# Attention in a transformer layer: tile 10 of the steady heads made in two parts, and one low part moved from GpSimd to VectorE

## The chip, the core and the metric

One core of one Trainium2 chip runs the whole program in one launch. The metric is the device time in microseconds (us). PE is TensorE, DVE is VectorE, ACT is ScalarE, POOL is GpSimd, and SP is the engine whose queue issues most of the transfers. The engines run beside each other, and only semaphores order them.

## The reference, cut to what matters

The layer is causal attention with 16 heads of width 32 over 2048 tokens, followed by a mixture of 16 experts. The change touches the attention alone:

```python
qkv = x @ W_qkv.T                       # x is layer-normed, 2048 x 512
q, k, v = jnp.split(qkv, 3, axis=-1)    # 16 heads of 32
attn = jnp.einsum('bhqd,bhkd->bhqk', q, k) * SCALE
attn = jnp.where(causal[None, None], attn, -jnp.inf)
probs = jax.nn.softmax(attn, axis=-1)
out = jnp.einsum('bhqk,bhkd->bhqd', probs, v)
```

All of it is float32.

## The kernel before, in words

PE multiplies in the format fp32r, which keeps fewer bits of a number than float32 does. A number x is therefore written as a high part (x copied to fp32r) and a low part (x minus its high part), and the products of the parts are summed.

**The tiles of a head.** A head has NS = 20 tiles (`S_TILES`, line 526). A tile is a pair of 128-key blocks against one block of 512 queries (j). Block j = 0 has tiles 0 and 1, j = 1 has 2 to 5, j = 2 has 6 to 11, j = 3 has 12 to 19. The last tile of a block (1, 5, 11, 19) covers 2x256 numbers in each partition, all others 2x512. Tile 10 is one that the causal mask cuts, so that its second key block needs only 384 of the 512 queries on PE.

**What happens to a tile.**
- PE makes the scores (`scores`, line 900: L911, and L915 for the mask) into one of two PSUM places.
- ACT takes the exponential into `prob` (L752), one of RING = 5 places.
- The high part `prob_hi` is made by ACT (L739), or by DVE (L796) for the tiles in `HI_DVE`.
- The low part `prob_lo` is made by POOL (L717) for the tiles in `LO_POOL`, otherwise by DVE (L803).
- PE multiplies both parts with the values (`times_v`, L893) LAG = 4 steps after the scores, so tile t's values stand in step t + 4, and those of tiles 16 to 19 in steps 0 to 3 of the next head. PE does the product with the high part first and the one with the low part after it.
- A tile in `WHOLE` has neither part: PE multiplies `prob` itself in float32 (L884).
- When all tiles of a query block are summed, ACT copies the sum out (`copy_out`, L733), PE turns it, DVE reads it (`read_out`, L788 and L789), and POOL scales it and stores it (`store_out`, L708). DVE's read of one block waits until POOL has stored the block before it.

**Beside it**, PE and DVE work on the next head's row maxima. PE makes 40 pieces of scores (L852, L855) into two PSUM places, and DVE reduces each (L767). `PIECES_AT` says how many pieces stand in each step: none in steps 0 to 4, two or three in each later one.

**Order.** Each engine has its own loop over the 20 steps, and its order is fixed by that code. In step t, DVE does the first pieces, then the high and low part of tile t - 1 if they are its own, then further pieces, then what `SHARED_AT` names for the step. So the low part of tile 17 would stand in DVE's step 18, ahead of the read of block 2 and of the two pieces of step 19. POOL goes through its own tiles in order, with the four stores between: block 3 of the head before after tile 6, block 0 after tile 9, block 1 after tile 15, block 2 after tile 18. Heads 0 to 14 use the sets `WHOLE`, `HI_DVE` and `LO_POOL` (head 0 written out, 1 to 14 in a loop). Head 15 has sets of its own, which are not changed.

Of the kernel before, what the change touches and what calls it, by code (L numbers as in the profile page):

```python
# [526 lines left out]
NS = len(S_TILES)  # L527
# [24 lines left out]
FW = VW + 1  # L552


WHOLE, WHOLE_LAST = {10}, {7, 17, 18}
HI_DVE, HI_DVE_LAST = {2, 3}, {1, 2, 3, 4, 5, 8, 9, 11, 13, 15, 19}
LO_POOL, LO_POOL_LAST = set(range(NS)) - {0, 1, 2, 18, 19} - WHOLE, {0}

def load_projection(sp, flat, wproj_dram, wgate_dram, landed):

# [1591 lines left out]
```

## Time and profile before

| | |
|---|---|
| median of three runs | 1682.74 us (1682.65 to 1682.8) |
| profiled execution | 1683.45 us, its span 1681.3 us |
| busy: PE, DVE, ACT, POOL | 1609.8, 1189.7, 1146.0, 907.0 us |
| granted TensorE clock, mean | 0.983 |
| POOL's low parts (L717) | 211 in 467.0 us, 2245 ns each on average |
| DVE's low parts (L803) | 91 of both sizes, in 111.3 us |

Attention runs from about 158 us to about 780 us of the span. A steady head takes 38.5 us there. Shares over the whole span say little about it, since the second half of the span is the expert stage, so the rows below are of steady heads.

### The profile page before, as it was taken

Reading aid. Unit: us, or ns where it says so; the run is one execution under the profiler, and the core shown is the slowest. Engines: PE = TensorE matmul, PEld = TensorE weight load, DVE = VectorE, ACT = ScalarE, POOL = GpSimd, SP = SyncE. Lnnn points to the kernel's source line nnn. Section 1 sums busy time; section 2 is a strip of 40 time slices with the busy share of each in tenths; the row PEclk is TensorE's granted clock in tenths of the full one; section 3 lists DMA queues with packets and bytes.
Section 4 is the critical chain, followed back from the end, with each engine's and each line's share of the span. In section 5 each row is a group of like instructions: output and inputs, shape, how many; then the busy total and the mean of one; then the engine's idle time right before and its main releaser. Section 6 shows DMA issues by size and latency. Waiting matters only on the chain.

```text
span 1681.3 us, 30901 instructions
## 1 busy us (share of the span) xinstructions
PE 1609.8 (96%) x9214; PEld 1360.1 (81%) x9214; DVE 1189.7 (71%) x2394; ACT 1146.0 (68%) x1729; POOL 907.0 (54%) x761
## 2 busy tenths in 40 slices
PE   7999999999999999999977999999999999999991
PEld 7988777777777777776756999999999999999991
DVE  6427888888888888887787667566665566556555
ACT  3222899999989999986776566566665565556554
POOL 2321788888888887874663443434343434343432
PEclk9999999999999999999988999999999999999996
DMA  8676221111111122212716898888887887788747
GB/s 254 188 222 186 63 67 51 50 50 50 50 50 50 51 71 71 59 48 88 267 48 237 234 283 243 230 257 237 240 254 216 223 259 213 205 253 235 195 111 219
DMA packets 103474, 268.21 MB, mean 160 GB/s; under 512 B 21129, under 2 KB 38921, under 8 KB 96073
## 3 DMA queue, kind: packets, MB, share of 16 engines
q1 hardware_dynamic: 77929, 204.64, 36.8%
q0 software_dynamic: 25440, 62.27, 18.2%
q8 instruction: 54, 0.88, 0.2%
q14 instruction: 51, 0.42, 0.1%
HBM read 190.55 MB, written 59.27 MB: 149 GB/s over the span
## 4 chain that ended last, share of the span: by engine, by line
PE 86%; DVE 6%; DMA 3%; issue 2%; ACT 1%; POOL 1%; SPq 1%; DVEq 0%; ACTq 0%; POOLq 0%
PE p_prj L91 26%; PE a_op L893 13%; PE a_sp L911 8%; PE a_mp L852 8%; PE p_at_ps L91 7%; PE p_logit_ps L91 7%; PE e_qp L91 5%; PE p_ht_ps L2031 3%; PE p_at_ps L2054 2%; PE e_vp L91 2%; PE a_op L884 2%; PE a_mp L855 1%; PE a_sp L915 1%; PE a_shared L870 1%; DVE r_lane_hot L1718 1%
## 5 line engine op out<-in xcount | busy, mean ns | idle before, releaser
L717 POOL TENSOR_TENSOR prob_lo<-prob,prob_hi 128x1024 fp32r<-128x1024 f32 (+1 forms) x211 | 467.0, 2245 | 120.5 <-DVE prob_hi L796 119.4
L767 DVE TENSOR_REDUCE part_max<-a_mp 128x1 f32<-128x512 f32 (+2 forms) x600 | 358.8, 609 | 79.5 <-PE a_mp L852 48.1
L1428 POOL DMA_INDIRECT acc_rows<-m_y_out,m_row_ids x108 | 175.2, 1622 | 401.2 <-ACT m_y_out L1587 254.3
L752 ACT ACTIVATE prob<-a_sp 128x1024 f32<-128x1024 f32 x320 | 292.5, 926 | 13.2 <-PE a_sp L911 10.7
L91 PE MATMUL p_prj<-m_w_hi,m_ht_hi 128*128 128x352 f32 x888 | 297.5, 335 | 1.8 <-DVE m_ht_lo L1827 1.5
L91 PE MATMUL p_prj<-m_w_lo,m_ht_hi 128*128 128x352 f32 x888 | 288.1, 324 | 0.0
L91 PE MATMUL p_prj<-m_w_hi,m_ht_lo 128*128 128x352 f32 x888 | 287.5, 324 | 0.0
L1851 DVE TENSOR_TENSOR m_w_lo<-m_w_raw,m_w_hi 128x704 fp32r<-128x704 f32 (+1 forms) x357 | 270.7, 797 | 23.4 <-ACT m_w_hi L1593 23.0
L739 ACT ACTIVATE prob_hi<-prob 128x1024 fp32r<-128x1024 f32 (+1 forms) x261 | 251.2, 962 | 8.3
L1593 ACT ACTIVATE m_w_hi<-m_w_raw 128x704 fp32r<-128x704 f32 (+1 forms) x357 | 229.0, 714 | 19.3 <-PE p_prj L91 16.8
L1837 DVE TENSOR_TENSOR m_at_lo<-p_at_ps,m_at_hi 128x384 fp32r<-128x384 f32 x111 | 61.8, 557 | 252.4 <-ACT m_at_hi L1579 252.4
L91 PEld LDWEIGHTS p_prj<-m_w_hi,m_ht_hi 128*128 128x128 f32 x888 | 167.6, 189 | 9.1 <-DVE m_ht_lo L1827 1.9
L91 PEld LDWEIGHTS p_prj<-m_w_lo,m_ht_hi 128*128 128x128 f32 x888 | 167.9, 189 | 4.8
L893 PE MATMUL a_op<-prob_hi,v_head 128*65 128x512 f32 (+1 forms) x604 | 169.8, 362 | 0.5 <-ACT o_sb L733 0.4
L893 PE MATMUL a_op<-prob_lo,v_head 128*65 128x512 f32 (+1 forms) x604 | 168.6, 360 | 0.5 <-DVE prob_lo L803 0.5
L91 PEld LDWEIGHTS p_prj<-m_w_hi,m_ht_lo 128*128 128x128 f32 x888 | 167.4, 188 | 0.0
L1420 POOL DMA_INDIRECT gathered<-h_rows,m_row_ids x108 | 113.2, 1048 | 43.2 <-issue 23.1
L1573 ACT ACTIVATE m_gate<-p_prj 128x352 f32<-128x352 f32 x111 | 51.6, 465 | 121.1 <-PE p_prj L91 121.1
L852 PE MATMUL a_mp<-k_stack,q_stack 96*128 96x512 f32 (+2 forms) x320 | 125.3, 391 | 1.6 <-DVE rows L418 0.8
L803 DVE TENSOR_TENSOR prob_lo<-prob,prob_hi 128x1024 fp32r<-128x1024 f32 (+1 forms) x91 | 111.3, 1250 | 0.9
L852 PE MATMUL a_mp<-multi 96*128 96x512 f32 (+2 forms) x280 | 109.4, 391 | 0.9 <-DVE part_max L767 0.3
L911 PE MATMUL a_sp<-multi 97*128 97x512 f32 (+1 forms) x320 | 106.1, 400 | 0.7 <-DMA v_head<-v_all 0.7
(259 smaller groups left out, 3245.4 us busy)
## 6 DMA issues: line engine op xcount, KB each, us to landing
m_w_raw<-wexp SPq DMA_DIRECT2D x51, 1408.0 KB, 7.0
m_w_raw<-wexp SPq DMA_DIRECT2D x51, 768.0 KB, 5.9
qk_parts<-rows SPq DMA_DIRECT2D x64, 256.0 KB, 3.2
multi<-qk_parts SPq DMA_DIRECT2D x84, 128.0 KB, 2.9
v_head<-v_all SPq DMA_DIRECT2D x16, 520.0 KB, 3.6
k_stack<-qk_parts SPq DMA_DIRECT2D x42, 128.0 KB, 2.6
q_stack<-qk_parts SPq DMA_DIRECT2D x42, 128.0 KB, 2.8
m_w_raw<-wexp SPq DMA_DIRECT2D x2, 2176.0 KB, 12.2
```

Source lines behind the costliest of these rows:

```text
L91: last = nc.tensor.matmul(out, a, b, start=c == n == 0, stop=c == chunks - 1 and n == 2)
L717: nc.gpsimd.tensor_tensor(prob_lo[:, t % RING, :, c0:NB], prob[:, t % RING, :, c0:NB], f32(prob_hi[:, t % RING, :, c0:NB]), ALU.subtract). ...
L739: nc.scalar.activation(prob_hi[:, t % RING, :, c0:NB], prob[:, t % RING, :, c0:NB], ACT.Copy).then_inc(hi_act, 1)
L752: nc.scalar.activation(prob[:, t % RING, :, c0:NB], sp_[:, t % 2, :, c0:NB], ACT.Exp, scale=SCALE).then_inc(prob_ready, 1)
L767: nc.vector.reduce_max(part_max[:, qb, kb:kb + 1], mp[:, n % 2, 0:width], AX_X).then_inc(piece_done, 1)
L852: last = nc.tensor.matmul(mp[:, n % 2, 0:k1 - k0], qs[p][0:K_ROWS, qb * P:(qb + 1) * P], ks[p][0:K_ROWS, k0:k1], start=True, stop=not diag ...
L893: last = nc.tensor.matmul(op[0:VW, cols], vs[p][:, 2 * kp + b, :], (prob_hi, prob_lo)[part][:, t % RING, b, cols], start=t == J_FIRST[j] a ...
L911: last = nc.tensor.matmul(sp_[:, t % 2, b, first:NB], ks[p][0:ROW_MAX + 1, kb * P:(kb + 1) * P], qs[p][0:ROW_MAX + 1, j * NB + first:(j + ...
L1420: nc.gpsimd.indirect_dma_start(gathered[:, t % 4, :], None, h_dram, bass.IndirectOffsetOnAxis(ap=row_id(t), axis=0)).then_inc(h_landed[t % ...
L1428: nc.gpsimd.indirect_dma_start(acc_dram, bass.IndirectOffsetOnAxis(ap=row_id(t), axis=0), y_out[:, t % 4, :], None, compute_op=ALU.add).th ...
L1593: nc.scalar.activation(w_hi[b % 2][:, a:z], raw_of(b)[:, a:z], ACT.Copy).then_inc(w_hi_done, 1)
L1851: nc.vector.tensor_tensor(w_lo[b % 2][:, a:z], raw_of(b)[:, a:z], f32(w_hi[b % 2][:, a:z]), ALU.subtract).then_inc(w_lo_done, 1)
```

## The change

Tile 10 is no longer in `WHOLE` in heads 0 to 14: ACT makes its high part, POOL its low part, and PE multiplies both. The low part of tile 17 is made by DVE instead of POOL.

```diff
-WHOLE, WHOLE_LAST = {10}, {7, 17, 18}
+WHOLE, WHOLE_LAST = set(), {7, 17, 18}
 HI_DVE, HI_DVE_LAST = {2, 3}, {1, 2, 3, 4, 5, 8, 9, 11, 13, 15, 19}
-LO_POOL, LO_POOL_LAST = set(range(NS)) - {0, 1, 2, 18, 19} - WHOLE, {0}
+LO_POOL, LO_POOL_LAST = set(range(NS)) - {0, 1, 2, 17, 18, 19} - WHOLE, {0}
```

POOL's instructions for the second half of head 0 (the steady heads have the same order with register work between). L717 is a low part, L708 a store; `128x2x256` is tile 11. Before:

```order
L717 TENSOR_TENSOR prob_lo<-prob,prob_hi 128x1024 x4
L708 TENSOR_TENSOR rows<-o_sum,recip 128x4x32
L717 TENSOR_TENSOR prob_lo<-prob,prob_hi 128x2x256
L717 TENSOR_TENSOR prob_lo<-prob,prob_hi 128x1024 x4
L708 TENSOR_TENSOR rows<-o_sum,recip 128x4x32
L717 TENSOR_TENSOR prob_lo<-prob,prob_hi 128x1024 x2
L708 TENSOR_TENSOR rows<-o_sum,recip 128x4x32
```

And now:

```order
L717 TENSOR_TENSOR prob_lo<-prob,prob_hi 128x1024 x4
L708 TENSOR_TENSOR rows<-o_sum,recip 128x4x32
L717 TENSOR_TENSOR prob_lo<-prob,prob_hi 128x1024
L717 TENSOR_TENSOR prob_lo<-prob,prob_hi 128x2x256
L717 TENSOR_TENSOR prob_lo<-prob,prob_hi 128x1024 x4
L708 TENSOR_TENSOR rows<-o_sum,recip 128x4x32
L717 TENSOR_TENSOR prob_lo<-prob,prob_hi 128x1024
L708 TENSOR_TENSOR rows<-o_sum,recip 128x4x32
```

Tile 10 stands ahead of tiles 11 to 16, and tile 17 is gone from the end.

DVE's instructions at the end of head 0 (steps 18 and 19). L767 is a piece, L788 and L789 are the read of block 2, L803 is a low part. Before:

```order
L780 TENSOR_SCALAR max_rows<-a_shared 12x128
L767 TENSOR_REDUCE part_max<-a_mp 128x1 x5
L788 RECIPROCAL recip<-a_shared 128x4
L789 TENSOR_REDUCE o_sum<-a_shared 128x128
L767 TENSOR_REDUCE part_max<-a_mp 128x1 x2
L803 TENSOR_TENSOR prob_lo<-prob,prob_hi 128x1024
```

And now:

```order
L780 TENSOR_SCALAR max_rows<-a_shared 12x128
L767 TENSOR_REDUCE part_max<-a_mp 128x1 x5
L803 TENSOR_TENSOR prob_lo<-prob,prob_hi 128x1024
L788 RECIPROCAL recip<-a_shared 128x4
L789 TENSOR_REDUCE o_sum<-a_shared 128x128
L767 TENSOR_REDUCE part_max<-a_mp 128x1 x2
L803 TENSOR_TENSOR prob_lo<-prob,prob_hi 128x1024
```

The new low part (tile 17) stands between the pieces and the read of block 2; the last row in both is tile 18.

PE's instructions of step 14 in a steady head, as a difference of the two kernels. `a_mp` is a piece, `a_op` the sum over the values:

```order
 L852 MATMUL a_mp<-k_stack,q_stack 128x128
 L855 MATMUL a_mp<-mask_q,ident_r 128x128
-L884 MATMUL a_op<-prob,v_head 65x512
+L893 MATMUL a_op<-prob_hi,v_head 65x512
+L893 MATMUL a_op<-prob_hi,v_head 65x384
 L852 MATMUL a_mp<-k_stack,q_stack 128x512
-L884 MATMUL a_op<-prob,v_head 65x384
+L893 MATMUL a_op<-prob_lo,v_head 65x512
+L893 MATMUL a_op<-prob_lo,v_head 65x384
 L911 MATMUL a_sp<-multi 128x512 x2
```

Two float32 products become four fp32r products, at the same places between the pieces.

## Rows read from the trace of the kernel before

**Rows 1.** The page: busy time of the engines over the whole span; engines on the last chain
```profile
PE 1609.8 (96%) x9214; PEld 1360.1 (81%) x9214; DVE 1189.7 (71%) x2394; ACT 1146.0 (68%) x1729; POOL 907.0 (54%) x761
PE 86%; DVE 6%; DMA 3%; issue 2%; ACT 1%; POOL 1%; SPq 1%; DVEq 0%; ACTq 0%; POOLq 0%
```

**Rows 2.** Windows, one steady head: stretch, its length, busy us by engine, TensorE clock
```profile
core 0: us, PE busy (x) PEld busy (x) DVE busy (x) ACT busy (x) POOL busy (x), PEclk, DMA share, GB/s
659.90:698.40 38.50, 38.42 (x212) 28.69 (x211) 33.31 (x61) 35.43 (x42) 32.27 (x19) 1.00 0.20 55
```

**Rows 3.** Waits in 14 steady heads (197.4 to 736.8 us): total us, times, longest
```profile
POOL prob_lo L717 <- DVE prob_hi L796: 86.2, 14, 6.2
...
PEld a_mp L852 <- DVE part_max L767: 15.9, 63, 0.5
...
PEld a_sp L911 <- ACT prob L752: 4.1, 16, 0.5
```

**Rows 4.** Timeline of PE, one steady head: start, us, engine, line, out<-in, shape, count
```profile
651.94 0.63 PE L893 MATMUL a_op<-prob_lo,v_head 128*65 128x512 f32 x2
...
653.35 1.02 PE L884 MATMUL a_op<-prob,v_head 128*65 128x512 f32 x2
654.44 0.81 PE L884 MATMUL a_op<-prob,v_head 128*65 128x384 f32 x2
...
666.65 0.62 PE L893 MATMUL a_op<-prob_lo,v_head 128*65 128x512 f32 x2
...
670.37 0.34 PE L893 MATMUL a_op<-prob_lo,v_head 128*65 128x256 f32 x2
```

**Rows 5.** Timeline of POOL, the same head; in brackets idle time before and its releaser
```profile
635.21 8.38 POOL L717 TENSOR_TENSOR prob_lo<-prob,prob_hi 128x1024 fp32r<-128x1024 f32 x4 [6.23 <-DVE prob_hi L796]
...
650.96 0.40 POOL L708 TENSOR_TENSOR rows<-o_sum,recip 128x128 f32 x1
651.32 10.72 POOL L717 TENSOR_TENSOR prob_lo<-prob,prob_hi 128x512 fp32r<-128x512 f32 x5
...
662.37 4.74 POOL L717 TENSOR_TENSOR prob_lo<-prob,prob_hi 128x1024 fp32r<-128x1024 f32 x2
667.07 0.39 POOL L708 TENSOR_TENSOR rows<-o_sum,recip 128x128 f32 x1
673.70 8.37 POOL L717 TENSOR_TENSOR prob_lo<-prob,prob_hi 128x1024 fp32r<-128x1024 f32 x4 [6.23 <-DVE prob_hi L796]
```

**Rows 6.** Timeline of DVE, the same head, step 18 to step 4 of the next
```profile
663.84 0.18 DVE L788 RECIPROCAL recip<-a_shared 128x4 f32<-128x4 f32 x1
...
664.58 1.45 DVE L767 TENSOR_REDUCE part_max<-a_mp 128x1 f32<-128x512 f32 x2 [0.25 <-PE a_mp L852]
665.95 2.60 DVE L803 TENSOR_TENSOR prob_lo<-prob,prob_hi 128x1024 fp32r<-128x1024 f32 x1
...
668.55 2.41 DVE L803 TENSOR_TENSOR prob_lo<-prob,prob_hi 128x512 fp32r<-128x512 f32 x3
...
671.60 1.22 DVE L803 TENSOR_TENSOR prob_lo<-prob,prob_hi 128x1024 fp32r<-128x1024 f32 x1
...
672.95 0.67 DVE L796 CAST prob_hi<-prob 128x1024 fp32r<-128x1024 f32 x1
```

**Rows 7.** Timeline of ACT, the same head: steps 12 and 15, and step 3 of the next
```profile
649.29 1.03 ACT L752 ACTIVATE prob<-a_sp 128x1024 f32<-128x1024 f32 x1 [0.69 <-PE a_sp L911]
...
656.71 0.59 ACT L733 ACTIVATE o_sb<-a_op 65x512 f32<-65x512 f32 x1 [1.29 <-PE a_op L893]
...
670.83 0.59 ACT L733 ACTIVATE o_sb<-a_op 65x512 f32<-65x512 f32 x1 [0.18 <-PE a_op L893]
671.32 1.93 ACT L752 ACTIVATE prob<-a_sp 128x1024 f32<-128x1024 f32 x2
```

**Rows 8.** Groups by shape, 14 steady heads: ACT's high parts
```profile
L739 ACT ACTIVATE prob_hi<-prob 128x1024 fp32r<-128x1024 f32 x183 | 194.1, 1061 | 5.8
```

**Rows 9.** Timelines of DVE and POOL in another head, the end of tile 17
```profile
281.20 2.26 DVE L803 TENSOR_TENSOR prob_lo<-prob,prob_hi 128x1024 fp32r<-128x1024 f32 x1
```

**Rows 10.** Timeline of POOL at the same place
```profile
277.63 4.76 POOL L717 TENSOR_TENSOR prob_lo<-prob,prob_hi 128x1024 fp32r<-128x1024 f32 x2
282.33 1.40 POOL L708 TENSOR_TENSOR rows<-o_sum,recip 128x128 f32 x1
```

## The prediction

> **What bounds the kernel now.** I read the page first. PE is busy 96% of the span and holds 86% of the last chain [rows 1], but that averages attention with the expert stage, which the change doesn't touch. So I took one steady head by itself. In its 38.50 us PE is busy 38.42, ACT 35.43, DVE 33.31 and POOL 32.27, at full clock [rows 2]. The waits say the same: over 14 heads PE waited 15.9 us for DVE's pieces and 4.1 us for exponentials, some 1.4 us a head, and never for POOL [rows 3]. PE sets the length of a head.
>
> By busy time POOL has 6.2 us to spare, but the timeline shows where they lie: in one gap, before tile 3, where POOL waits for the high part that DVE makes [rows 3, 5]. From there POOL runs without a pause. Its slack is therefore not 6.2 us but the distance between the end of each low part and PE's use of it. One full low part takes 4.74 / 2 = 2.37 us [rows 5]. Tile 9's is ready at 650.96 and used at 651.94 (1.0 to spare); tile 16's is ready at 662.37 + 2.37 = 664.74 and used at 666.65 (1.9 to spare) [rows 4, 5].
>
> **PE's own part.** The two float32 products of tile 10 take 1.02 and 0.81 us [rows 4]. A pair of 512-column fp32r products takes 0.62 [rows 4], and the pairs overlap by their ends; with 512 + 384 columns the two pairs come to some 1.2 us. That is 1.83 - 1.2 = about 0.6 us less; since the pieces between them still need DVE, I take 0.4 to 0.7 us a head as PE's gain, if nothing else holds it.
>
> **ACT's own part.** One more high part of 1.06 us [rows 8], between the exponentials of tiles 10 and 11. ACT waits 0.69 us before tile 12's exponential and 1.29 us before the copy of block 2 [rows 7], 1.98 together, so the 1.06 fits in, and with PE's gain too (1.06 + 0.7 = 1.76). Cost: nothing. Without that cover it would be 1.06 us a head.
>
> **POOL's part.** The number of low parts is unchanged, 14 a head, so a look at the sums says zero. But tile 10 stands ahead of 11 to 16. After the store at 650.96 to 651.36 come tile 10 (2.37) and the old run of 10.72, so tile 15 ends at 651.32 + 2.37 + 10.72 = 664.41, the store of block 1 lasts to 664.77, and tile 16's low part ends at 662.37 + 2 x 2.37 = 667.11 instead of 664.74. PE used it at 666.65 and hoped for about 666.0. Dropping tile 17 frees POOL only behind tile 16, where it had the gap anyway. Tiles 10 to 14 just meet PE.
>
> Does that late arrival come round again in the next head? The loop is: POOL starts tile 3 (635.21), tile 16 ready (667.11), 31.90 us. PE from the low part of tile 16 to the end of tile 19 is 666.65 to 670.71, 4.06 us without a gap [rows 4]. Then ACT copies block 3 out 0.12 later (670.83), takes tile 3's exponential 0.49 after that start, for about 1.0 [rows 7], DVE makes its high part (0.67, and 0.08 to POOL's start) [rows 5, 6]. With 0.2 for the hand-over from POOL to PE: 31.90 + 0.2 + 4.06 + 0.12 + 0.49 + 1.0 + 0.67 + 0.08 = 38.52 us. That is exactly the old 38.5. So with no price at all for DVE's new work, PE's gain is already gone.
>
> **DVE's part.** A low part on DVE costs 1.22 us alone [rows 6], but 2.60 at 665.95, while POOL was in tile 17 [rows 5, 6]. 665.95 + 2.60 - 1.22 = 667.33: DVE began only when POOL's tile 17 (to 667.11) had ended, and the small store behind it had started at 667.07 too. The two do not run beside each other. It is so in all 15 heads (2.26 to 2.98 us). Who goes first when POOL has its next instruction ready can be seen too: in 14 of the 15 heads POOL's store went ahead of the waiting DVE. In one DVE went first: 281.20 + 2.26 - 1.22 = 282.24, before POOL's tile ended at 282.39, and the store took 1.40 instead of 0.39 us [rows 9, 10], 1.0 late.
>
> Tile 17's low part will stand ready on DVE at about 663.2 to 663.9, where the read of block 2 stands now (663.84) [rows 6]. POOL is then in tile 15 (to 664.41), with the store of block 1 and tile 16 behind it and no gap. If POOL wins at both borders, as in 14 of 15, DVE waits until tile 16 ends, and all that stands behind on DVE waits too: the read of block 2, two pieces, the low parts of 18, 19, 0, 1, the high part of 2, the low part of 2, then the high part of 3, which starts POOL.
> - DVE gets through at 667.0 (the 282.39 - 282.24 = 0.15 before the recorded end), done 668.2.
> - Read and two pieces: 663.84 to 665.95 is 2.11, less 0.25 of idle [rows 6], so tile 18's low part starts 1.85 after 668.1 (each starts 0.1 before its forerunner's end): 669.95. POOL's store is over by then. It ends 671.15.
> - Tile 19's starts at 671.1 to 671.2 instead of 668.55, 2.55 late. From there to POOL's start DVE works without a gap (668.55 to 673.62) [rows 6], so all of it is passed on.
> - PE's chain is earlier: tile 18 used at 671.3, the end of 19 at 672.7, tile 3's exponential over by 674.3, before DVE comes to it at 675.5.
>
> So a head becomes 38.5 + 2.55 = 41.05 us. Tile 10 is split in 15 heads, and each hands the delay on. 15 x 2.55 = 38.3 us. SP's order doesn't change, and its loads land long before they are wanted.
>
> **The sum.** 1683.45 (the profiled execution) + 38.3 = 1721.7; the median of the runs shown lies 0.7 below that execution, so 1721.
>
> **Rivals.**
> - *DVE gets in between POOL's instructions.* If DVE takes its turn before or after the store of block 1, the low part costs POOL the 1.0 us of rows 10, and tile 16 ends at 668.1. The loop is 38.52 + 1.0 = 39.5. DVE, past its low part at 665.8, meets tile 16 with tile 18's part, waits till 668.2, ends at 669.4: 0.9 late, the same 39.5. 15 x 1.0 = 15 us: 1698. For it: DVE has waited longest, the store is short, and one head in 15 shows it. Against it: the 14.
>  The Trainium skill (SBUF — State Buffer, "SBUF: two separate sides") says that GpSimd and a VectorE instruction with two SBUF inputs share a port pair as an exclusive lock, and that whoever starts first has it for the whole instruction. The 2.60 against 1.22 us [rows 6] agree. If that were first come, first served, this rival would be the outcome, +15 us; 14 of the 15 borders say otherwise.
> - *No price on DVE.* If the tile 17 part met POOL without waiting, the loop is 38.52: no change, 1683. Against it: all 15 heads show the wait. For it: the hand-overs in my loop are estimates of 0.1 to 0.2 us, and mixed heads could recover a part.
> - *PE stays the bound and keeps its gain* (the other side). Then 15 x 0.4 to 0.7 = 6 to 10 us less, about 1675. It needs tile 16's low part at PE by 666.0 on the old clock, 1.1 us sooner than POOL can have it. The point from which it decides is a POOL part under 2.37 - 1.1 / 7 = 2.2 us for each of the seven from tile 10 to 16. What speaks for it is PE's 38.42 of 38.50; against it, that PE's slack to POOL was never over 1.9 us at tile 16 and the change takes 2.37.
>
> **How the numbers follow.** Chances: POOL wins both borders 0.52, DVE gets in between 0.26, no price 0.13, PE keeps its gain 0.09. The predicted time is that of the first, 1721; its own range is 1708 to 1728 (2 to 3 us a head, with some heads of the other kind). To hold 8 in 10 the range must reach down over the second and third case: 1682 to 1728, which leaves out the gain and a small tail above. 0.2% (3.4 us) is about what a measurement can tell from no change. Slower by more than that: 0.52 + 0.26 and a little of the third, 0.79; the same 0.13; faster 0.08.
>
> **What the changed profile would show.** Steady heads of about 41 us; DVE's low part of tile 17 lasting 3.5 to 4.5 us, where 1.2 would be alone, and ending 1.1 us after POOL's tile 16; PE waiting for `prob_lo` from DVE and POOL, which it never did for POOL; POOL's gap before tile 3 near 7.3 us instead of 6.2, with a new one of 1.5 us ahead of the store of block 2; no float32 products in heads 0 to 14, and step 14 about half a microsecond shorter. Heads of 39.5 us with POOL's tile 16 at 3.4 us would show the first rival; heads under 38.5 with tile 16's low part ahead of PE would refute the step on POOL's order.

## The result and the profile after

The changed kernel takes 1720.17 us (median of 6 runs, 1718.2 to 1721.1) against 1682.7 us (6 runs) for the kernel before: the ratio is 1.022, 95% interval 1.0208 to 1.0232. It is slower by 2.2%. Forecast were 1721 us and a range of 1682 to 1728.

Start with the windows. One steady head of the changed kernel, cut from one start of POOL's tile 3 to the next; columns as in [rows 2]:

```profile
core 0: us, PE busy (x) PEld busy (x) DVE busy (x) ACT busy (x) POOL busy (x), PEclk, DMA share, GB/s
665.19:706.01 40.82, 38.26 (x210) 28.38 (x210) 36.57 (x61) 36.66 (x43) 32.26 (x19) 1.00 0.18 52
```

A head takes 40.82 us instead of 38.5 [rows 2]. POOL's busy time did not move (32.26 against 32.27), ACT's grew by 1.23, and DVE's by 3.26 us, of which only 1.22 is the work of one low part; "busy" counts a DVE low part also while it waits for POOL. PE is idle for 2.56 us, where it was idle for 0.08 before. No sum of busy times comes near 40.82: the head has to be found in a loop that runs through several engines.

POOL in that head (it answers to [rows 5]; in brackets idle time and its releaser):

```profile
665.19 8.37 POOL L717 TENSOR_TENSOR prob_lo<-prob,prob_hi 128x1024 fp32r<-128x1024 f32 x4 [6.81 <-DVE prob_hi L796]
...
681.29 13.06 POOL L717 TENSOR_TENSOR prob_lo<-prob,prob_hi 128x1024 fp32r<-128x1024 f32 x6
694.31 0.40 POOL L708 TENSOR_TENSOR rows<-o_sum,recip 128x128 f32 x1
694.67 2.38 POOL L717 TENSOR_TENSOR prob_lo<-prob,prob_hi 128x1024 fp32r<-128x1024 f32 x1
698.71 0.40 POOL L708 TENSOR_TENSOR rows<-o_sum,recip 128x128 f32 x1 [1.67 <-DVE o_sum L789]
706.01 8.36 POOL L717 TENSOR_TENSOR prob_lo<-prob,prob_hi 128x1024 fp32r<-128x1024 f32 x4 [6.89 <-DVE prob_hi L796]
```

Read it from POOL's start at 665.19. Tile 16's low part ends at 694.67 + 2.38 = 697.05, 31.86 after the start; before it was 29.53. The run is gapless up to there, and then two gaps stand where one stood: 1.67 us in which POOL waits for DVE's read of block 2, and 6.89 before tile 3.

DVE in the same stretch (it answers to [rows 6]; where rows are merged, the shape is that of the first, so the `x3` are tiles 19, 0 and 1):

```profile
691.72 1.40 DVE L767 TENSOR_REDUCE part_max<-a_mp 128x1 f32<-128x512 f32 x2 [0.35 <-PE a_mp L852]
693.04 5.09 DVE L803 TENSOR_TENSOR prob_lo<-prob,prob_hi 128x1024 fp32r<-128x1024 f32 x1
698.05 0.17 DVE L788 RECIPROCAL recip<-a_shared 128x4 f32<-128x4 f32 x1
...
699.65 1.21 DVE L803 TENSOR_TENSOR prob_lo<-prob,prob_hi 128x1024 fp32r<-128x1024 f32 x1
...
700.86 2.41 DVE L803 TENSOR_TENSOR prob_lo<-prob,prob_hi 128x512 fp32r<-128x512 f32 x3
...
705.26 0.67 DVE L796 CAST prob_hi<-prob 128x1024 fp32r<-128x1024 f32 x1
```

The second row is the low part of tile 17. It lasts 5.09 us, 1.22 of them work, and ends at 698.13. Take off 1.22 and it began at 696.91, 0.14 before POOL's tile 16 is recorded to end. POOL crossed two borders meanwhile, tile 15 to the store (694.31) and the store to tile 16 (694.67), and DVE got in at neither. Tile 17's high part (ACT) had ended at 692.53, so nothing else held it: beside the semaphores, the two engines order each other by excluding each other. It is so in all 15 heads: the row lasts 4.52 us in head 0 and 5.08 to 5.20 in the others. Everything behind it is late. Tile 19's low part starts at 700.86, 35.67 after POOL's start, where it was 33.34; from there to POOL's next start are 5.15 us, as before.

The waits of heads 0 to 14 (200 to 760 us; they answer to [rows 3]):

```profile
POOL rows L708 <- DVE o_sum L789: 24.1, 14, 2.0
PEld a_op L893 <- POOL prob_lo L717: 21.5, 26, 1.5
...
PEld a_op L893 <- DVE prob_lo L803: 19.1, 14, 1.4
```

PE waits for POOL's and for DVE's low parts. Steady heads had neither row before. PE's waits are where the time shows, not where it is made.

PE's own gain is in the trace too. These are the products of tile 10 in step 14, and the first product of tile 11 behind them, now and then before:

```profile
683.32 0.57 PE L893 MATMUL a_op<-prob_hi,v_head 128*65 128x512 f32 x2
...
683.97 0.56 PE L893 MATMUL a_op<-prob_lo,v_head 128*65 128x512 f32 x2
...
685.01 0.34 PE L893 MATMUL a_op<-prob_hi,v_head 128*65 128x256 f32 x2
```

```profile
655.72 0.34 PE L893 MATMUL a_op<-prob_hi,v_head 128*65 128x256 f32 x2
```

From the start of tile 10's products to tile 11's are 685.01 - 683.32 = 1.69 us now; before they were 655.72 - 653.35 = 2.37 [rows 4]. PE has its 0.68 us, and the head is 2.3 us longer all the same.

The stretches add up. From POOL's first tile 3 to its last one (14 heads) are 571.37 us now and 538.33 before, 33.0 more or 2.36 a head. The end of attention behind it is 2.3 us longer, and 1.7 us lie ahead of attention, where nothing was changed. Together 37.0, against spans that differ by 36.7.

### The profile page after: what moved, and what is told of

Read it like the earlier page. It is cut to its first block, busy times and chain, and to the rows that moved or that the text cites. A ratio compares the mean times of both kernels' runs of the same rounds, so it can differ in the third digit from the quotient of the medians.

```text
span 1718.0 us, 30973 instructions
## 1 busy us (share of the span) xinstructions
PE 1605.5 (93%) x9214; PEld 1356.2 (79%) x9214; DVE 1237.3 (72%) x2409; ACT 1165.1 (68%) x1744; POOL 903.6 (53%) x761
## 4 chain that ended last, share of the span: by engine, by line
PE 77%; DVE 11%; issue 6%; DMA 2%; ACT 1%; POOL 1%; DVEq 1%; SPq 0%; POOLq 0%; ACTq 0%
PE p_prj L91 25%; PE a_op L893 9%; PE a_mp L852 7%; PE p_at_ps L91 7%; PE p_logit_ps L91 7%; PE a_sp L911 6%; PE e_qp L91 5%; DVE prob_lo L803 4%; PE p_ht_ps L2031 3%; PE e_vp L91 3%; DVE part_max L767 2%; PE p_at_ps L2054 2%; PE a_mp L855 1%; DVE r_lane_hot L1718 1%; PE a_shared L870 1%
## 5 line engine op out<-in xcount | busy, mean ns | idle before, releaser
L717 POOL TENSOR_TENSOR prob_lo<-prob,prob_hi 128x1024 fp32r<-128x1024 f32 (+1 forms) x211 | 466.5, 2243 | 128.9 <-DVE prob_hi L796 95.8
L767 DVE TENSOR_REDUCE part_max<-a_mp 128x1 f32<-128x512 f32 (+2 forms) x600 | 355.5, 608 | 66.4 <-PE a_mp L852 39.6
L739 ACT ACTIVATE prob_hi<-prob 128x1024 fp32r<-128x1024 f32 (+1 forms) x276 | 267.1, 968 | 8.8
L893 PE MATMUL a_op<-prob_lo,v_head 128*65 128x512 f32 (+1 forms) x634 | 178.9, 363 | 29.0 <-DVE prob_lo L803 15.6
L893 PE MATMUL a_op<-prob_hi,v_head 128*65 128x512 f32 (+1 forms) x634 | 177.9, 362 | 3.0 <-ACT o_sb L733 1.3
L803 DVE TENSOR_TENSOR prob_lo<-prob,prob_hi 128x1024 fp32r<-128x1024 f32 (+1 forms) x106 | 168.2, 1609 | 0.9
L893 PEld LDWEIGHTS a_op<-prob_lo,v_head 128*65 128x65 f32 x634 | 76.5, 137 | 71.1 <-POOL prob_lo L717 23.6
```

Source lines behind the costliest of these rows:

```text
L717: nc.gpsimd.tensor_tensor(prob_lo[:, t % RING, :, c0:NB], prob[:, t % RING, :, c0:NB], f32(prob_hi[:, t % RING, :, c0:NB]), ALU.subtract). ...
L739: nc.scalar.activation(prob_hi[:, t % RING, :, c0:NB], prob[:, t % RING, :, c0:NB], ACT.Copy).then_inc(hi_act, 1)
L767: nc.vector.reduce_max(part_max[:, qb, kb:kb + 1], mp[:, n % 2, 0:width], AX_X).then_inc(piece_done, 1)
L803: nc.vector.tensor_tensor(prob_lo[:, t % RING, :, c0:NB], prob[:, t % RING, :, c0:NB], f32(prob_hi[:, t % RING, :, c0:NB]), ALU.subtract). ...
L893: last = nc.tensor.matmul(op[0:VW, cols], vs[p][:, 2 * kp + b, :], (prob_hi, prob_lo)[part][:, t % RING, b, cols], start=t == J_FIRST[j] a ...
```

## The experiments

Below, "the loop" is: POOL starts tile 3; runs its low parts without a gap; DVE, which cannot run a low part beside POOL's, makes tile 18's when POOL is through; DVE's gapless rest (19, 0, 1, the high part of 2, the low part of 2, a copy of maxima, the high part of 3); POOL starts tile 3. Each kernel was timed beside the kernel before on one chip; ratios are to that. A length of heads is the mean of 13 steady ones between POOL's starts of tile 3; by that measure it is 38.47 us in the kernel before and 40.84 in the changed one.

### Each half of the change alone

Tile 10 split, tile 17 left on POOL:

```diff
-LO_POOL, LO_POOL_LAST = set(range(NS)) - {0, 1, 2, 17, 18, 19} - WHOLE, {0}
+LO_POOL, LO_POOL_LAST = set(range(NS)) - {0, 1, 2, 18, 19} - WHOLE, {0}
```

> Only the first half of the change: tile 10 in two parts, tile 17's low part stays on POOL. Theory (the loop POOL tile 3 to tile 17, DVE tile 18 to the high part of tile 3, in which POOL goes ahead of a waiting DVE): POOL's tiles 10 to 17 all end 2.37 us later, so tile 17 ends at start + 31.9 + 2.37 = 34.3; DVE's low part of tile 18 waits for that and for the store, ends at about 35.7 instead of 33.34, so a head becomes 38.5 + 2.35 = 40.85 us and the program about 1718. So half of the change alone costs nearly as much as the whole. Rival A (the price is the new instruction on DVE, tile 17): without it only tile 16's lateness is left, heads of 38.5 to 38.6, 1683 to 1685. Rival B (PE is the bound and keeps its gain once DVE is relieved): 1673 to 1677.

Measured: 1721.4 us, ratio 1.0224 (1.0207 to 1.0241), 3 us above the theory's 1718. Heads of 40.88 us (forecast 40.85). One of them, POOL (which started tile 3 at 624.30) and then DVE:

```profile
653.80 4.71 POOL L717 TENSOR_TENSOR prob_lo<-prob,prob_hi 128x1024 fp32r<-128x1024 f32 x2
658.47 0.40 POOL L708 TENSOR_TENSOR rows<-o_sum,recip 128x128 f32 x1
```

```profile
653.93 0.18 DVE L788 RECIPROCAL recip<-a_shared 128x4 f32<-128x4 f32 x1 [1.72 <-POOL rows L708]
655.54 4.41 DVE L803 TENSOR_TENSOR prob_lo<-prob,prob_hi 128x1024 fp32r<-128x1024 f32 x1
```

Tile 18's low part on DVE now bears the wait: 4.41 us, and it ends at 659.95, 1.08 behind the end of POOL's store (658.87). So the split alone costs as much as the whole change, and rival A (the price is the new DVE instruction) and rival B fall. Moving tile 17 to DVE neither adds to the loss nor takes from it: POOL is through 2.4 us sooner, and DVE has 1.2 us of work and a queue behind it instead.

The other half, tile 10 whole and tile 17 on DVE:

```diff
-WHOLE, WHOLE_LAST = set(), {7, 17, 18}
+WHOLE, WHOLE_LAST = {10}, {7, 17, 18}
```

> Only the second half: tile 10 stays whole, tile 17's low part goes to DVE. Theory: POOL ends tile 16 at start + 29.5, DVE comes to tile 17 at 28.6, waits 0.8, ends at 30.6; read of block 2 and two pieces bring tile 18's part to a start at 32.4 with the port free, end 33.6 instead of 33.34: heads of 38.5 to 38.8, 1683 to 1687. Rival A (a low part moved to DVE costs its own 1.2 us and what stands behind it, wherever POOL is): 39.7 a head, 1701 or more. Rival B (PE alone sets the head): no change, 1683.

Measured: 1683.35 us, ratio 1.0001 (0.9992 to 1.0011). No change.

```profile
664.56 2.03 DVE L803 TENSOR_TENSOR prob_lo<-prob,prob_hi 128x1024 fp32r<-128x1024 f32 x1
...
668.12 1.21 DVE L803 TENSOR_TENSOR prob_lo<-prob,prob_hi 128x1024 fp32r<-128x1024 f32 x1
```

POOL started at 636.02 here. Tile 17's part waits 0.8 us and tile 18's ends at 669.33, 33.31 after the start: the same as the 33.34 before. A low part moved to DVE is free where POOL's run ends soon after DVE asks, and dear where it doesn't.

### DVE's wait taken away

No low part of tile 17 at all in heads 0 to 14, with PE's two products of it left out:

```diff
+NO_LOW = {17}
...
-            if t in lo_pool_tiles(h) | whole_tiles(h):
+            if t in lo_pool_tiles(h) | whole_tiles(h) or t in NO_LOW and lo_pool_tiles(h) is LO_POOL:
                 return
...
+                if no_low and part:
+                    return
```

> The changed kernel without tile 17's low part in heads 0 to 14: no engine makes it and PE leaves out its two products (so that part of the sum is missing). It takes away exactly the wait on DVE. Theory: what is left is POOL's order. Tile 16 ends at start + 31.9, PE's run from there is 0.46 shorter (4.06 to 3.60), so the loop over PE is 38.06; over DVE tile 18's low part waits until POOL's tile 16 and store are over (32.1) and ends at 33.3: 38.45. Heads of 38.1 to 38.5, 1677 to 1683. Rival (tile 16's lateness is the main cost, not DVE's wait): heads of 39.5 and more, 1698 or more. Rival (PE sets the head): 38.5 - 0.6 - 0.46 = 37.4, 1666.

Measured: 1684.17 us, ratio 1.0004 (0.9994 to 1.0014), a microsecond above the forecast, heads of 38.47. PE's waits for POOL's low parts (200 to 735 us):

```profile
PEld a_op L898 <- POOL prob_lo L719: 19.6, 16, 1.5
```

The whole loss is gone, although tile 16's low part is as late as in the changed kernel (31.88 after POOL's start) and PE still waits for it, up to 1.5 us as there. So it is DVE's work and wait, not PE's wait for tile 16, that costs 2.4 us a head. And PE, with tile 10's products shortened and the two of tile 17's low part gone, is busy 37.30 us of a head of 38.49 (the one from 599.40) and gains nothing: the loop is back at its old length and holds it.

### Who goes first at a border

The low part of tile 10 on DVE, in step 11, in the middle of POOL's run:

```diff
-LO_POOL, LO_POOL_LAST = set(range(NS)) - {0, 1, 2, 17, 18, 19} - WHOLE, {0}
+LO_POOL, LO_POOL_LAST = set(range(NS)) - {0, 1, 2, 10, 18, 19} - WHOLE, {0}
```

> Tile 10 in two parts, its low part on DVE in step 11, tile 17's on POOL: the DVE low part now stands in the middle of POOL's gapless run. It tells who goes first at the borders. Theory (POOL goes ahead as long as it has a ready instruction): DVE is shut out from about start + 13.3 until POOL runs out of ready tiles, which happens only because PE stops for want of pieces; DVE's instruction lasts 7 to 10 us, a head 44 to 47 us, the program 1765 to 1810. Rival (first come, first served): DVE gets in at the next border, its instruction lasts 1.5 to 3.5 us, POOL loses 1.0 once, heads of 39.5 us, 1698.

Measured: 1814.75 us, ratio 1.0775 (1.0752 to 1.0797). POOL, DVE and PE:

```profile
616.18 0.40 POOL L708 TENSOR_TENSOR rows<-o_sum,recip 128x128 f32 x1
616.54 5.87 POOL L717 TENSOR_TENSOR prob_lo<-prob,prob_hi 128x512 fp32r<-128x512 f32 x3
630.56 2.40 POOL L717 TENSOR_TENSOR prob_lo<-prob,prob_hi 128x1024 fp32r<-128x1024 f32 x1 [8.15 <-ACT prob_hi L739]
```

```profile
614.83 8.65 DVE L803 TENSOR_TENSOR prob_lo<-prob,prob_hi 128x1024 fp32r<-128x1024 f32 x1
```

```profile
671.81 0.80 PE L852 MATMUL a_mp<-k_stack,q_stack 96*128 96x512 f32 x1 [7.48 <-DVE part_max L767]
```

DVE asks at 614.83 and ends at 623.48; less 1.22 is 622.26, 0.15 before POOL's three low parts end (622.41). In between POOL went from tile to tile, to a store and on, and DVE got in nowhere. It was let in only when POOL had nothing ready, because PE stood still for want of DVE's pieces (the third fence, one head later). At these borders first come, first served falls. The wait is inside the forecast's 7 to 10 us; the head (47.78 us here, 47.89 in the mean) and the program are a little longer than the 44 to 47 us and the 1765 to 1810 us expected.

But "POOL goes ahead as long as it has a ready instruction" doesn't hold either. Later in the same head DVE waits with the low part of tile 18, at the border from POOL's tile 17 to the store of block 2:

```profile
640.67 1.94 DVE L803 TENSOR_TENSOR prob_lo<-prob,prob_hi 128x1024 fp32r<-128x1024 f32 x1
```

```profile
641.49 1.39 POOL L708 TENSOR_TENSOR rows<-o_sum,recip 128x128 f32 x1
```

640.67 + 1.94 - 1.22 = 641.39: DVE went first, and the store, recorded from 641.49 without a gap behind tile 17, took 1.39 instead of 0.40 us, as in [rows 10]. So it is in 13 of the 15 heads of this run. At this one place DVE went first in 1 of 15 heads of the kernel before, in 13 of 15 here and in 9 of 15 of a run further down, and in none with the split alone or with tile 10's low part left out. DVE had been waiting for 0.8 to 1.4 us where it won, and for 0.8 to 3.0 us where it lost in these five kernels, so the length of the wait alone doesn't decide. Where the next POOL instruction was a low part that followed without a gap, POOL went first every time.

In the head from 600.46 the mean granted clock is 0.89 instead of 1.00. It fell while PE stood still, and from 624.0 to 629.2 PE worked at a granted clock of 0.52, that is almost all at the lower of its two levels. An estimate of what that costs: PE is busy 40.20 us in this head and 38.79 in one of the split alone (from 583.47), so some 1.4 us of the 9.4 a head.

### What set the head before the change

Tile 10 split but its low part left out, POOL and DVE as before:

```diff
+NO_LOW = {10}
...
-LO_POOL, LO_POOL_LAST = set(range(NS)) - {0, 1, 2, 17, 18, 19} - WHOLE, {0}
+LO_POOL, LO_POOL_LAST = set(range(NS)) - {0, 1, 2, 10, 18, 19} - WHOLE, {0}
```

> Tile 10 in two parts but without its low part: no engine makes it and PE leaves out its two products in heads 0 to 14 (that part of the sum is missing); tile 17's low part stays on POOL. PE has some 1.0 to 1.1 us less a head than before, POOL and DVE do exactly what they did before. It asks what set the head before the change. Theory (the loop POOL tile 3 to 17, DVE tile 18 to the high part of tile 3, is as long as a head by itself): no gain, heads of 38.4 to 38.5, 1680 to 1684. Rival (PE alone sets the head, as its 38.42 busy us of 38.50 say): heads of 37.4, 1666 to 1669.

Measured: 1684.4 us, ratio 1.0012 (1.0002 to 1.0021), at the upper end of the forecast, heads of 38.51. One stretch of the length of a head:

```profile
650.00:688.50 38.50, 37.60 (x210) 28.12 (x209) 34.11 (x60) 36.40 (x43) 32.27 (x19) 1.00 0.19 55
```

PE has 0.8 us less to do than in [rows 2], and the head is 38.52 us (from 637.65 to 676.17 between POOL's starts). The rival, that PE alone set the head, falls. PE's 38.42 of 38.50 and a loop of the same length stood side by side in the kernel before.

### The order on DVE

One instruction of the changed kernel moved: tile 17's low part behind the read of block 2 and the two pieces of step 19.

```diff
+LATE = (17,)
...
+                if t == NS - 1 and not last:
+                    for late in LATE:
+                        low_part(h, late)
-                if t >= 1:
+                if t >= 1 and (last or t - 1 not in LATE):
                     low_part(h, t - 1)
```

> The changed kernel with one line moved: DVE makes tile 17's low part just ahead of tile 18's, behind the read of block 2 and the two pieces of step 19, so these no longer stand behind its wait. Theory: the read waits only for POOL's store of block 1 (start + 29.6), the pieces end at 31.3, tile 17's part waits for POOL's tile 16 and the store behind it (32.1) and ends at 33.3, tile 18's at 34.5 instead of 33.34: heads of 38.47 + 1.15 = 39.6, 1700. Rival (the loss is in PE's wait for tile 16's low part, which is unchanged): heads stay at 40.8, 1718 to 1720.

Measured: 1701.93 us, ratio 1.0111 (1.0096 to 1.0127), heads of 39.63 (forecast 39.6). DVE's rows:

```profile
680.22 0.18 DVE L789 RECIPROCAL recip<-a_shared 128x4 f32<-128x4 f32 x1 [1.80 <-POOL rows L709]
681.82 3.20 DVE L804 TENSOR_TENSOR prob_lo<-prob,prob_hi 128x1024 fp32r<-128x1024 f32 x2
```

Half of the loss was not the low part but what stood behind it while it waited. POOL's order is untouched, so this half can't be PE's wait for tile 16.

### Versions meant to be faster

Both with tile 17's part late on DVE (the edit above), and a tile of half the width left whole: tile 11, or tile 5. The first of them:

```diff
-WHOLE, WHOLE_LAST = set(), {7, 17, 18}
+WHOLE, WHOLE_LAST = {11}, {7, 17, 18}
```

> A version meant to be faster than both: tile 17's part late on DVE, and tile 11 (half as wide, 384 columns on PE) is the whole one instead of tile 10 (896 columns). PE has 0.2 to 0.4 us less a head than before, ACT 0.43 more in steps that have slack. Theory: POOL has tile 10 for tile 11, 1.07 more, and not tile 17, so tile 16 ends at start + 30.6 and its store at 31.0; the pieces of step 19 end at 30.3 to 30.7, tile 17's part at 32.1, tile 18's at 33.2 instead of 33.34. The loop is 38.2 to 38.4, PE needs 38.1: 1678 to 1683. Rival (DVE's added 1.2 us is paid in full, since it has no gap before tile 18): heads of 39.0 or more, 1690 or more.

> The same with tile 5 as the whole one (also half as wide), in step 9, where PE and ACT have no slack by the trace, instead of tile 11 in step 15. Theory: POOL's run is as long as with tile 11 (tile 16 ends at start + 30.6), so it should come out the same within 3 us: 1678 to 1684. Rival (where the float32 product stands on PE matters more than POOL's run): 5 us or more from the run with tile 11.

Measured: 1682.65 us, ratio 0.9995 (0.9986 to 1.0004), with tile 11; 1683.15 us, ratio 1.0001 (0.9992 to 1.001), with tile 5. Both inside the forecasts, both no gain that can be told. Heads are 38.39 and 38.38 us. DVE's 1.2 us are paid by POOL's shorter run; whether tile 11 or tile 5 is whole doesn't matter.

Next, DVE's copy of the second maxima (0.20 us in the loop) moved behind the high part of tile 3, once with tile 11 whole and once in the kernel before:

```diff
                 if t >= 1:
                     high_part(h, t - 1)
+                    if t == 4 and not last:
+                        if not first:
+                            maxima_out(h, "b")
...
-                if what == "max_b" and not first:
+                if what == "max_b" and not first and last:
                     maxima_out(h, "b")
```

> The version with tile 11 whole and tile 17's part late, and on DVE the copy of the second maxima (0.20 us in the chain) now stands behind the high part of tile 3 instead of ahead of it. Theory (the loop over POOL and DVE still sets the head): it gets 0.20 us shorter, 38.36 to 38.16, 15 x 0.2 = 3 us: 1679 to 1680. Rival (by now PE or ACT sets the head): no change from 1682.7.

> The kernel before with only that copy moved behind the high part of tile 3. Theory: the loop goes from 38.47 to 38.27, but PE's own order with its float32 product is about as long, so 0 to 3 us are gained: 1679.7 to 1682.7. Rival (the kernel before was bound by PE alone): 1682.7, no change at all.

Measured: 1680.09 us with tile 11 whole, ratio 0.9973 (0.9962 to 0.9985), faster than the kernel before by 0.27% and than the changed one by some 2.4% (0.9973 / 1.022), heads of 38.20 us. In the kernel before, the same edit gives 1683.29 us, ratio 0.9997 (0.9988 to 1.0006), heads of 38.44. Two starts of tile 3 with tile 11 whole:

```profile
633.77 8.35 POOL L718 TENSOR_TENSOR prob_lo<-prob,prob_hi 128x1024 fp32r<-128x1024 f32 x4 [7.19 <-DVE prob_hi L797]
...
671.96 8.35 POOL L718 TENSOR_TENSOR prob_lo<-prob,prob_hi 128x1024 fp32r<-128x1024 f32 x4 [7.18 <-DVE prob_hi L797]
```

The loop's 0.2 us are worth something only where PE has been shortened too: PE is busy 37.91 us in a head of the first (from 595.57) and 38.38 of 38.45 in one of the second (from 596.39). Together with the run without tile 10's low part this shows two bounds of equal length in the kernel before: shortening either alone brings nothing.

The kernel before with the moved copy is also the one in which DVE went first at the store of block 2 in 9 of 15 heads. DVE, then POOL:

```profile
665.91 2.04 DVE L803 TENSOR_TENSOR prob_lo<-prob,prob_hi 128x1024 fp32r<-128x1024 f32 x1
```

```profile
666.83 1.39 POOL L708 TENSOR_TENSOR rows<-o_sum,recip 128x128 f32 x1
```

The mean head is 38.44 us all the same, so in this kernel it costs nothing who goes first at this border.

Last, tile 2's low part on DVE moved behind the high part of tile 3 as well:

```diff
+                        low_part(h, 2)
...
-                if t >= 1 and (last or t - 1 not in LATE):
+                if t >= 1 and (last or t - 1 not in LATE + (2,)):
```

> As the first of these, and DVE also makes tile 2's low part behind the high part of tile 3. POOL may then start tile 3 about a microsecond sooner, at the moment when DVE asks for its low part of tile 2. Theory (the one that asks first on a free port gets it, and DVE's own next instruction is ready first): DVE's low part goes ahead, POOL's first instruction lasts 1.1 us longer, the head is 38.2 to 38.4, 1680 to 1683. Rival (POOL goes ahead of DVE always): DVE's low part of tile 2 is shut out for most of POOL's run, and the pieces behind it with it: heads of 45 us or more, over 1780.

Measured: 1686.89 us, ratio 1.0012 (1.0003 to 1.0021), heads of 38.78. DVE, then POOL:

```profile
674.53 0.68 DVE L797 CAST prob_hi<-prob 128x1024 fp32r<-128x1024 f32 x1
676.02 0.69 DVE L797 CAST prob_hi<-prob 128x1024 fp32r<-128x1024 f32 x1 [0.82 <-ACT prob L753]
676.63 1.22 DVE L804 TENSOR_TENSOR prob_lo<-prob,prob_hi 128x1024 fp32r<-128x1024 f32 x1
```

```profile
676.79 3.30 POOL L718 TENSOR_TENSOR prob_lo<-prob,prob_hi 128x1024 fp32r<-128x1024 f32 x1 [6.83 <-DVE prob_hi L797]
```

Who goes first came out as the theory had it: with POOL idle, DVE asked 0.16 us sooner and went first, and POOL's first low part took 3.30 instead of 2.37 us, in all 14 steady heads. POOL has no standing priority. The size was wrong. I had the head at 38.2 to 38.4: DVE now reaches the high part of tile 3 before ACT has its exponential, waits 0.82 us, and the low part it could have made in that time stands behind.

## Why the prediction was right

- *What bounds the kernel.* "PE sets the length of a head" was half of it. The loop of 38.52 us that the prediction worked out was, it wrote, exactly the old 38.5, and it concluded rightly that PE's gain was gone. It didn't draw the further conclusion that the loop bound the kernel before as well. The two runs that left out a low part (tile 17's, tile 10's) and the moved copy show that it did.
- *PE's own part.* 0.4 to 0.7 us a head. Held: step 14's products of tile 10 take 0.68 us less in the changed kernel, and the products themselves 0.57 + 0.56 = 1.13 us instead of 1.83. In none of these kernels was it worth anything by itself.
- *ACT's part at nothing.* Held: in the two runs that left out a low part ACT makes tile 10's high part and is busy 36.4 us, and the heads are 38.47 and 38.51 us, as long as before.
- *POOL's part.* Tile 16's end was forecast at 31.9 after the start: 31.86. As forecast, POOL's busy time stayed where it was and the gap was no reserve.
- *DVE's part.* Forecast: shut out at both borders, let in 0.15 before tile 16 ends, 2.55 us late for tile 19's part. Measured: both borders in 15 of 15 heads, 0.14, and 35.67 - 33.34 = 2.33 late. The 0.2 us between lie in what stands behind it. I put the read and the pieces at 1.85 us, and the rows have 699.65 - 698.05 = 1.60. The instruction itself lasts longer than the 3.5 to 4.5 us forecast (5.1). That range didn't follow from the prediction's own steps: ready at 663.2 to 663.9 and done at 668.2 are 4.3 to 5.0 us. The rest is that DVE was a little earlier at its place (27.85 after POOL's start, where the steps have 28.0 to 28.7). What counts for the head is when it ends, and that was 32.94 after the start against 32.99.
- *The sum.* 15 x 2.55 = 38.3 against 14 x 2.36 and 2.3, 35.3; the 1.7 us ahead of attention belong to the execution and not to the change, and brought the total closer to the forecast than its terms were. That much of the agreement is luck.
- *The first rival* (DVE gets in between) was given 0.26. It did not happen in a single head: POOL went first at 30 of 30 borders. But the evidence that the prediction went by, 14 of 15, was weaker than it looked. It came from the border before the store of block 2, and small moves in time turned that into 6 and 2 of 15 (the moved copy, tile 10's low part on DVE). The store's inputs were ready in the heads that I looked at: in that of [rows 9, 10] DVE's read had ended at 279.58, and the store could start at 282.33. The mechanism, POOL first at both borders, was right; that the one border foretold the others was in part luck, and what decides at a border stays open.
- *What was missed.* DVE's read of block 2 waits for POOL's store of block 1, which tile 10 makes 2.4 us later. It hides behind the low part of tile 17 in the changed kernel, but in the split alone it is a row of its own (1.72 us a head).

## What to carry to other kernels

An engine's idle time in a gapless run counts only at the place where it lies: measure the slack of each of its results to its user, and follow the loop through all engines for one round. An instruction that can't run beside another engine's must stand where that engine is about to run out of work, with nothing urgent queued behind it. One low part made by DVE cost nothing where it waited 0.8 us for the end of POOL's run (tile 17, with tile 10 whole) and 9.4 us a head in the middle of the run (tile 10); with POOL's run 2.4 us longer, tile 17's cost 2.4 us and half of that in a later place. When a shortened engine brings nothing, look for a second loop of the same length and shorten both.

## What the hardware showed that I had not expected

A waiting DVE instruction with two SBUF inputs was shut out over 8.65 us and several borders while POOL's tensor instructions followed each other without a gap. With POOL idle, 0.16 us of lead were enough for DVE to go first, and then POOL waited inside its instruction (3.30 instead of 2.37 us). Where both wanted to go at a border, POOL mostly won, but not by a rule that these runs show: ahead of the store of block 2 DVE went first in 1, 9 and 13 of 15 heads of three kernels. DVE's instruction, less its 1.22 us, starts some 0.14 us before POOL's is recorded to end. The Trainium skill (SBUF — State Buffer, "SBUF: two separate sides") calls the port pair an exclusive lock that the one that starts first holds for the whole instruction. The case of 3.30 us agrees: DVE had started first, and POOL's low part stood still until DVE's was nearly over.
